# A decoder of two layers on one core: byte codes for four of sixteen heads in a quantised cross-attention, and a later schedule around them

## The chip, the cores and the metric

The kernel runs on one core of a Trainium2 chip. The metric is the device time of the whole program in microseconds, from one launch. Six sublayers are computed in that launch; the change touches mainly the fifth.

## The reference, cut to what matters

`x` is 4 x 256 rows of 256 numbers, so 1,024 queries; `cond` (the context) has as many rows, all of which are keys for every query. There are 16 heads of 16 numbers. What the fifth sublayer computes:

```python
x = x + attn0(ln(x)); x = x + xattn0(ln(x), ctx, ctx); x = x + bitlinear_ffn(ln(x)); x = x + latent_attn(ln(x))
# the fifth: quantised cross-attention
q = (ln(x) @ Wq + bq).reshape(1, B * N, 16, 16) / 4
k, v = split((cond @ Wkv + bkv).reshape(1, -1, 2, 16, 16))
q = fq_sym(q, axis=-1); k = fq_sym(k, axis=-1); v = fq_sym(v, axis=2)   # whole numbers to 127, times a scale
attn = softmax(einsum('bhqd,bhkd->bhqk', q, k))
attn = fq_unsigned(attn, axis=-1)   # round(attn / max * 255), times a scale
x = x + einsum('bhqk,bhkd->bhqd', attn, v).reshape(B, N, C) @ Wp + bp
x = x + moe(ln(x))                  # 32 experts and 32 empty ones, the best 8 of 64 for each token
```

With the row's largest score subtracted and ln 255 added, the exponential rounded to a whole number is the code from 0 to 255 of `fq_unsigned`. The scale drops out with the division by the row's sum.

## The kernel before

Each engine has its own instruction list, written out by hand, with semaphores between them. The fifth sublayer is a loop over units. Unit `n` is one tile of 128 queries (`q = n // 16`, eight tiles) and one head (`h = n % 16`), 128 units in all; 16 units, one tile, are called a round below. In a unit:

- TensorE multiplies the queries with all 1,024 keys: two matmuls of 128x512 (L1204) into one of three pairs of PSUM banks. It waits until the exponential of unit n-3 has been read out of that pair.
- VectorE takes the negated maximum of the 1,024 scores of each row (L1739). The bias of the exponential, that maximum times a scale plus ln 255, is one tiny instruction: VectorE does it for half of the units (L1746), GpSimd (`score_bias`, L619) for the units in `PBIAS`.
- ScalarE takes the exponential and writes the codes as int16 (L876) to one of `YB` buffers `Y5`; it reads out the row sums with it.
- SP issues a DMA transpose of the 128x1024 codes (L453), so that keys lie on partitions, into one of `YB` buffers `PT5`. The codes' bits are then read as float16.
- TensorE multiplies them with the values: eight matmuls with 16 columns (L1214). These are `LAG5` = 6 units behind: TensorE's list has the scores of unit n and then the value products of unit n-6.

In the free places of the loop lies the work on other tiles, hung on `at_unit(n, h)`, which is true h units after a tile's lag (n - LAG5 = 16 q + h). For tile q+2, which is still to come: the output projection of the fourth sublayer (`WO_H` = 4, TensorE L1117), its residual and statistics on VectorE (L1562, L1566, L1568), the norm on GpSimd (`ln_rstd` L589 and L591, `ln_apply` L596), the transpose, the query projection (`Q5_H` = 10), the quantising (`quantise_queries`), a DMA transpose (`query_T`, L440) and the padding of the queries (`pad_queries`, two copies, L627). For tile q-1, which is finished: the division (L1755, L1757), the output projection (`WP_H` = 6, TensorE L1129), the residual, statistics and norm, `store_rows` (L445) and the router's logits. Where a unit has no such work, TensorE multiplies an identity to keep busy (L1262).

Order in the lists matters, since each engine works its own list in order. GpSimd's for a unit n is the bias if n is in `PBIAS`, then, at their units, the norm of the later tile, the padding, the norm of the finished tile, the bias vector of the residual (L601) and the quantising. SP's is the transpose of the codes, then at its unit `store_rows` or `query_T`. VectorE's is the maximum and bias, then the side work. After the last unit come the router (the first six tiles are routed while the last value products run), the lists of tokens for each expert, and the experts.

The third sublayer quantises its hidden tile in five small steps on VectorE (L1479 to L1490) and then tells TensorE with a counter of its own, `qh_ready` (L1492), that it may transpose (L1025).

## Time and profile before

| what | value |
|---|---|
| median of three runs | 571.26 us (570.69 to 577.84) |
| the profiled execution | 572.61 us |
| its span in the trace | 570.9 us |
| busy over the span: PE, DVE, ACT, POOL | 78%, 76%, 57%, 44% |
| the loop of the fifth sublayer, first to last exponential | 237.2 to 434.9 us |
| median time of one DMA transpose of codes, issue to landing | 3.3 us |

The profiled execution is 1.35 us above the median of the runs; its span is 1.7 us shorter than its own time. Busy shares are over all stages. The loop is a third of the span, and the page's 40 slices show DVE at 7 to 9 tenths, ACT at 7 to 9 and DMA at 9 in it.

### The profile page before, as it was taken

What the parts mean: (1) busy time and instruction counts of PE and PEld (TensorE: products, weight loads), DVE (VectorE), ACT (ScalarE), POOL (GpSimd) and SP (SyncE); (2) the same over time, 40 slices, a digit from 0 to 9 for tenths busy, and PEclk for the clock granted to TensorE, in tenths of its full rate; (3) what the DMA queues carried; (4) which work ended last, traced back from release to release, by engine and by line L of the source; (5) the groups of instructions that cost most, each with busy time, mean ns of one, the idle gap of its engine ahead of it and who ended that gap; (6) DMA issues with size and microseconds to landing.
All of it is one profiled execution on the core that took longest, in us unless ns stands there. A gap on an engine that the chain in (4) does not pass through costs nothing.

```text
span 570.9 us, 10775 instructions
## 1 busy us (share of the span) xinstructions
PE 445.7 (78%) x3776; PEld 280.1 (49%) x3776; DVE 431.9 (76%) x892; ACT 322.7 (57%) x607; POOL 250.2 (44%) x367
## 2 busy tenths in 40 slices
PE   2999796677888888578888777787787877877775
PEld 1534562445555566244444444444434436766664
DVE  4697799889689877999999897999798753412246
ACT  1333434545578456488897887889795114434430
POOL 5645210005089466022536263543312148888860
PEclk9996897999899999898999999999799999999999
DMA  8760000000004202299999999999999978995456
GB/s 283 223 242 0 1 2 1 0 1 2 0 1 113 38 1 30 47 181 171 176 191 179 186 180 174 172 181 193 178 185 155 296 229 206 267 229 94 87 84 209
DMA packets 186149, 74.03 MB, mean 130 GB/s; under 512 B 159120, under 2 KB 183632, under 8 KB 186096
## 3 DMA queue, kind: packets, MB, share of 16 engines
q1 hardware_dynamic: 179968, 64.30, 54.2%
q0 software_dynamic: 5040, 8.00, 7.7%
q10 hardware_dynamic: 1088, 1.05, 0.6%
q8 instruction: 30, 0.49, 0.4%
q14 instruction: 23, 0.19, 0.1%
HBM read 27.69 MB, written 7.88 MB: 62 GB/s over the span
## 4 chain that ended last, share of the span: by engine, by line
PE 31%; DVE 23%; issue 16%; POOL 12%; ACT 9%; DMA 7%; SPq 0%; POOLq 0%; DVEq 0%; ACTq 0%
DVE nm L1739 5%; DMA A<-A 5%; DVE AT L1554 5%; ACT A L876 5%; POOL A L675 4%; PE ps L938 3%; POOL sums L685 3%; PE ps L955 3%; PE ps L1129 2%; PE ps L1204 2%; PE ps L1013 2%; PE ps L956 2%; PE ps L1117 2%; PE ps L1031 1%; ACT A L768 1%
## 5 line engine op out<-in xcount | busy, mean ns | idle before, releaser
L876 ACT ACTIVATE A<-ps,b,sq 128x1024 int16<-128x1024 f32 x128 | 153.6, 1205 | 39.2 <-DVE b L1746 24.8
L1739 DVE TENSOR_REDUCE nm<-ps 128x1 f32<-128x1024 f32 x128 | 152.6, 1211 | 6.9 <-PE ps L1204 6.6
L1204 PE MATMUL ps<-big,ctx_sb 128*128 128x512 bf16 x256 | 80.6, 398 | 33.0 <-ACT A L876 30.0
L1214 PEld LDWEIGHTS ps<-VI,A 128*128 128x128 f16 x1024 | 41.5, 97 | 53.6 <-DMA A<-A 34.3
L619 POOL TENSOR_SCALAR b<-nm,sq 128x1 f32<-128x1 f32 x61 | 16.3, 267 | 109.7 <-DVE nm L1739 100.8
L1214 PE MATMUL ps<-VI,A 128*128 128x16 f16 x1024 | 45.2, 170 | 13.7 <-DMA A<-A 13.0
L1811 DVE TENSOR_TENSOR AT<-AT,ps 128x128 f32<-128x128 f32 x32 | 9.2, 288 | 59.0 <-ACT AT L892 48.7
L1204 PEld LDWEIGHTS ps<-big,ctx_sb 128*128 128x128 bf16 x256 | 18.8, 100 | 57.7 <-ACT A L876 44.3
L675 POOL DMA_INDIRECT A<-x_rows,slot_token x32 | 34.9, 1091 | 23.7 <-DVE big L1731 14.2
L685 POOL DMA_INDIRECT sums<-XN,slot_token x24 | 38.7, 1614 | 8.1 <-issue 7.0
L1322 PE MATMUL ps<-A 128*128 128x128 f32 x256 | 34.8, 279 | 3.8 <-issue 1.8
L1262 PE MATMUL ps<-big,identb 128*128 128x256 bf16 x192 | 36.4, 280 | 0.0
L524 POOL TENSOR_SCALAR veps<-mv 128x4 f32<-128x4 f32 x8 | 2.1, 257 | 76.3 <-DVE mv L1360 76.3
L1322 PEld LDWEIGHTS ps<-A 128*128 128x128 f32 x256 | 31.1, 191 | 6.5 <-issue 6.2
L886 ACT ACTIVATE A<-ps 128x256 f32<-128x256 f32 x32 | 12.3, 383 | 38.6 <-PE ps L1312 32.4
L1554 DVE TENSOR_REDUCE AT<-ps 128x4 f32<-128x512 f32 (+1 forms) x32 | 27.8, 950 | 0.4 <-PE ps L1104 0.4
L921 PE MATMUL ps<-identb 128*128 128x512 bf16 x114 | 27.7, 379 | 0.0
L837 ACT ACTIVATE A<-ps 128x768 f32<-128x768 f32 x22 | 16.6, 808 | 15.6 <-PE ps L1143 15.6
L876 ACT ACTIVATION_READ_ACCUMULATOR A<-ps,b,sq 128x1 f32 x128 | 25.3, 198 | 0.0
L1299 PE MATMUL ps<-big 128*128 128x256 bf16 x192 | 23.9, 273 | 0.3 <-DVE big L1805 0.3
L1312 PE MATMUL ps<-identf,A 128*128 128x128 f32 x64 | 13.3, 290 | 13.7 <-DMA A<-x_rows,slot_token 12.8
L606 POOL TENSOR_SCALAR_AFFINE_SELECT A<-A 128x512 f32<-128x512 f32 x22 | 15.5, 708 | 13.9 <-ACT A L837 13.2
(305 smaller groups left out, 1044.9 us busy)
## 6 DMA issues: line engine op xcount, KB each, us to landing
A<-in SPq DMA_DIRECT2D x32, 256.0 KB
A<-in SPq DMA_DIRECT2D x32, 128.0 KB
A<-in SPq DMA_DIRECT2D x2, 1024.0 KB, 14.3
sums<-zeros SPq DMA_DIRECT2D x4, 512.0 KB, 5.0
A<-A SPq DMA_TRANSPOSE x128, 3.3
X<-in SPq DMA_DIRECT2D x1, 1024.0 KB, 6.0
big<-in SPq DMA_DIRECT2D x1, 1024.0 KB, 8.7
ctx_sb<-in SPq DMA_DIRECT2D x1, 1024.0 KB, 13.0
```

Of the source, the lines that this page charges most:

```text
L675: g.indirect_dma_start(out=XE[:, e % 8, :], out_offset=None, in_=x_rows, in_offset=bass.IndirectOffsetOnAxis(ap=slot_token[:, e:e + 1], ax ...
L685: g.indirect_dma_start(out=sums[j % 2], out_offset=bass.IndirectOffsetOnAxis(ap=slot_token[:, e:e + 1], axis=0), in_=YE[:, e % 8, :], in_o ...
L876: a.activation(Y5[:, n % YB, :], ps[:, 2 * ((n + 1) % 3):2 * ((n + 1) % 3) + 2, :], ACT.Exp, scale=sq5[:, q, h:h + 1], bias=b5[:, n % 4:n ...
L921: T.matmul(ps[:, bank, :], identb[:, :], identb[:, :].unsqueeze(1).to_broadcast([P, 4, P]), start=True, stop=True)
L938: last = T.matmul(ps[:, bank, 0:n], XT[:, k, t * P:(t + 1) * P], w[:, k, 0:n], start=(k == 0), stop=(k == KD - 1))
L1204: done = T.matmul(ps[:, 2 * ((n + 1) % 3) + c, :], QT5[:, q % 2, h // 2, h % 2, :], KT5[:, h // 2, c * 512:(c + 1) * 512], start=True, sto ...
L1214: done = T.matmul(ps[:, 6 + q % 2, h * HD:(h + 1) * HD], PT5h[:, m % YB, k, :], VI[:, k, h * HD:(h + 1) * HD], start=(k == 0), stop=(k == 7))
L1262: T.matmul(ps[:, 6 + q % 2, D:2 * D], identb[:, :], KT5[:, 0, 0:D], start=True, stop=True)
L1299: done = T.matmul(ps[:, 4 + c, (t % 2) * D:(t % 2 + 1) * D], HOT[:, i % 2, t * P:(t + 1) * P], YP[:, i % 2, a, :], start=(i == 0 and a == ...
L1322: last = T.matmul(ps[:, 1, f * P:(f + 1) * P], WG[:, e % WS, k, f * P:(f + 1) * P], XET[:, e % 2, k, :], start=(k == 0), stop=(k == KD - 1))
L1554: v.tensor_reduce(MM4[:, 2 * b + t, :].rearrange("p (r c) -> p r c", r=4)[:, :, HD + g], sc[:, :, lo:hi], AX.X, ALU.max, negate=True).then ...
L1739: v.tensor_reduce(nm5[:, n % 4:n % 4 + 1], ps[:, 2 * ((n + 1) % 3):2 * ((n + 1) % 3) + 2, :].rearrange("p a c -> p (a c)"), AX.X, ALU.max, ...
```

## The change

Four heads of each tile, h in `PACK_H` = (2, 4, 6, 13), so 32 of 128 units, write their codes as bytes. The exponential's output is ordered so that a key of one half of a 256-block and its partner 128 further on lie side by side; a pair of bytes is one 2-byte element. The DMA transpose then has 128x512 elements in place of 128x1024 and goes to one of two buffers `PK5`. GpSimd's new `unpack(m)` waits for it and copies the bytes out to the int16 buffer `PT5`, 1,024 elements for each partition, read with a stride of two bytes. It stands in GpSimd's list at n = m + 5, ahead of that unit's bias. TensorE waits for it in place of the DMA.

Further: `YB` and `LAG5` go from 6 to 8, so everything hung on `at_unit` and `PBIAS` moves two units later. VectorE's residuals and GpSimd's norms after the two projections go one unit further (`WO_H + 1`, `WP_H + 1`), while TensorE's projections stay at `WO_H` and `WP_H`. `pad_queries` goes from `WP_H` (6) to 2. In the third sublayer two semaphores are saved by counting on in others, which also removes VectorE's wait and increment of `qh_ready`. The logits' buffer moves in SBUF.

```diff
-YB, LAG5 = 6, 6
+YB, LAG5 = 8, 8
+        Y5b = A[:, 4096:4096 + 512 * YB].bitcast(U8).rearrange("p (b c) -> p b c", b=YB)
+        PK5 = A[:, 13312:13824].bitcast(I16).rearrange("p (s k c) -> p s k c", s=2, k=4)
+        PK5b = A[:, 13312:13824].bitcast(U8).rearrange("p (s k c a) -> p s k c a", s=2, k=4, a=2)
+        PACK_H = (2, 4, 6, 13)
+        PACKED = [n for n in range(U5) if n % H in PACK_H]
 # SP
-                sp.dma_start_transpose(PT5[:, n % YB, :, :], Y5[:, n % YB, :]).then_inc(p5T_loaded[n % YB], 16)
+                if n in PACKED:
+                    j = PACKED.index(n)
+                    if j >= 2:
+                        sp.wait_ge(S["p5U_ready"], j - 1)
+                    sp.dma_start_transpose(PK5[:, j % 2, :, :], Y5[:, n % YB, 0:512]).then_inc(p5T_loaded[n % YB], 16)
+                else:
+                    sp.dma_start_transpose(PT5[:, n % YB, :, :], Y5[:, n % YB, :]).then_inc(p5T_loaded[n % YB], 16)
 # GpSimd
+            def unpack(m):
+
+                j = PACKED.index(m)
+                pool.wait_ge(p5T_loaded[m % YB], 16 * (m // YB + 1))
+                if m >= YB:
+                    pool.wait_ge(S["p5V_done"], m - YB + 1)
+                g.tensor_copy(PT5[:, m % YB, :, :].rearrange("p (k a) c -> p k a c", k=4), PK5b[:, j % 2, :, :, :].rearrange("p k c a -> p k a c")).then_inc(S["p5U_ready"], 1)
-            for n in range(LAG5, U5 + LAG5 + H):
+            for n in range(LAG5 - 1, U5 + LAG5 + H):
+                if n - 5 in PACKED:
+                    unpack(n - 5)
                 if n in PBIAS:
                     score_bias(n)
-                if at == WO_H and ahead:
+                if at == 2 and 1 <= q < NT - 1:
+                    pad_queries(q + 1, n)
+                if at == WO_H + 1 and ahead:
                     ln_rstd("q", q + 2, q + 3)
                     ln_apply("q", q + 2)
-                if at == WP_H:
-                    if 1 <= q < NT - 1:
-                        pad_queries(q + 1, n)
+                if at == WP_H + 1:
 # ScalarE
-                    a.activation(Y5[:, n % YB, :], ps[:, 2 * ((n + 1) % 3):2 * ((n + 1) % 3) + 2, :], ACT.Exp, scale=sq5[:, q, h:h + 1],
+                    codes, scores = Y5[:, n % YB, :], ps[:, 2 * ((n + 1) % 3):2 * ((n + 1) % 3) + 2, :]
+                    if n in PACKED:
+                        codes = Y5b[:, n % YB, 0:1024].rearrange("p (k c a) -> p k a c", k=4, a=2)
+                        scores = scores.rearrange("p x (k a c) -> p (x k) a c", k=2, a=2)
+                    a.activation(codes, scores, ACT.Exp, scale=sq5[:, q, h:h + 1],
 # TensorE
-                    pe.wait_ge(S["qh_ready"], u + 1)
+                    pe.wait_ge(S["qh_step"], 2 * u + 2)
-                    pe.wait_ge(p5T_loaded[m % YB], 16 * (m // YB + 1))
+                    if m in PACKED:
+                        pe.wait_ge(S["p5U_ready"], PACKED.index(m) + 1)
+                    else:
+                        pe.wait_ge(p5T_loaded[m % YB], 16 * (m // YB + 1))
 # VectorE
-                    dve.wait_ge(S["qh_step"], 2 * s + 2)
-                    dve.sem_inc(S["qh_ready"], 1)
-                if at_unit(n, WO_H) is not None and q + 2 < NT:
+                if at_unit(n, WO_H + 1) is not None and q + 2 < NT:
                     side_residual(q + 2, bank, 0, "wo_psum", "xo_ready")
                     side_stats("q", q + 2, "xo_ready", q + 3)
-                if at_unit(n, WP_H) is not None and q >= 1:
+                if at_unit(n, WP_H + 1) is not None and q >= 1:
                     dve.wait_ge(S["xbias_ready"], q)
                     side_residual(q - 1, bank, D, "wp_psum", "xp_ready")
```

## Rows read from the trace of the kernel before

**Rows 1.** Windows, six rounds: us, busy PE, PEld, DVE, ACT, POOL, clock, DMA.

```profile
253.00:404.00 151.00, 118.39 (x1210) 68.38 (x1207) 137.72 (x206) 126.88 (x221) 64.41 (x119) 0.97 1.06 180
```

**Rows 2.** Timeline of SP's queue, 269 to 399 us: start, length, line, operation.

```profile
269.94 1.30 SPq L440 DMA_TRANSPOSE KV<-kpart  x1
...
295.36 1.28 SPq L440 DMA_TRANSPOSE KV<-kpart  x1
...
320.32 1.81 SPq L440 DMA_TRANSPOSE KV<-kpart  x1
322.22 17.43 SPq L453 DMA_TRANSPOSE A<-A  x12
339.70 0.57 SPq L445 DMA_DIRECT2D x_rows<-XN  x1
...
372.78 1.28 SPq L440 DMA_TRANSPOSE KV<-kpart  x1
...
397.44 1.46 SPq L440 DMA_TRANSPOSE KV<-kpart  x1
```

**Rows 3.** One line's instructions, L453: min/median/max ns; then us to landing.

```profile
L453 SPq DMA_TRANSPOSE A<-A x128: 1231/1285/2516, 238.6 to 437.7; - x128
...
DMA to landing us min/median/max: 3.1/3.3/5.9
```

**Rows 4.** Groups by line, 260 to 433 us: busy us, mean ns, idle before.

```profile
L876 ACT ACTIVATE A<-ps,b,sq 128x1024 int16<-128x1024 f32 x110 | 132.0, 1205 | 28.5 <-DVE b L1746 15.2 <-POOL b L619 10.0 <-DMA A<-A 1.9
L1739 DVE TENSOR_REDUCE nm<-ps 128x1 f32<-128x1024 f32 x110 | 131.0, 1211 | 6.7 <-PE ps L1204 6.6
...
L1214 PE MATMUL ps<-VI,A 128*128 128x16 f16 x880 | 38.9, 170 | 11.4 <-DMA A<-A 10.9
...
L619 POOL TENSOR_SCALAR b<-nm,sq 128x1 f32<-128x1 f32 x56 | 15.0, 267 | 89.9 <-DVE nm L1739 81.0 <-ACT A L876 8.9
...
L627 POOL COPY ctx_sb<-KV 64x1024 bf16<-64x1024 bf16 x12 | 12.4, 1036 | 0.7
...
L639 POOL TENSOR_SCALAR kpart<-ktmp 128x256 bf16<-128x256 f32 x6 | 6.6, 1102 | 0.6
...
L1562 DVE TENSOR_TENSOR X<-X,ps 128x256 f32<-128x256 f32 x12 | 5.0, 418 | 5.8 <-PE ps L1117 3.8 <-PE ps L1129 1.9
...
L641 POOL COPY kpart<-kpart 128x512 bf16<-128x512 bf16 x6 | 3.7, 612 | 0.4
```

**Rows 5.** Timeline of DVE around the residual of a later tile.

```profile
298.00 1.22 DVE L1739 TENSOR_REDUCE nm<-ps 128x1 f32<-128x1024 f32 x1
299.97 0.42 DVE L1562 TENSOR_TENSOR X<-X,ps 128x256 f32<-128x256 f32 x1 [0.76 <-PE ps L1117]
...
300.99 1.20 DVE L1739 TENSOR_REDUCE nm<-ps 128x1 f32<-128x1024 f32 x1
```

**Rows 6.** Timeline of PE in the same stretch.

```profile
297.96 1.97 PE L1117 MATMUL ps<-woT,A 128*128 128x256 f32 x8
299.77 0.59 PE L1204 MATMUL ps<-big,ctx_sb 128*128 128x512 bf16 x2
```

**Rows 7.** Timeline of POOL in the same stretch.

```profile
301.16 0.23 POOL L589 TENSOR_SCALAR veps<-mv 128x1 f32<-128x1 f32 x1 [1.59 <-DVE mv L1568]
...
302.15 1.24 POOL L596 TENSOR_SCALAR XN<-X,mv,rstd 128x256 f32<-128x256 f32 x1
...
303.99 2.13 POOL L627 COPY ctx_sb<-KV 64x1024 bf16<-64x1024 bf16 x2
```

**Rows 8.** The page's costliest groups, an exponential that writes four bytes an element.

```profile
L837 ACT ACTIVATE A<-ps 128x768 f32<-128x768 f32 x22 | 16.6, 808 | 15.6 <-PE ps L1143 15.6
```

**Rows 9.** Timeline of DVE after the last unit.

```profile
440.65 0.21 DVE L1666 MATCH_REPLACE8 ctx_sb<-top,ctx_sb 128x64 f32<-128x64 f32 x1
441.37 0.25 DVE L1755 RECIPROCAL r<-sum 128x16 f32<-128x16 f32 x1 [0.51 <-PE ps L1214]
```

**Rows 10.** One line's instructions, L1025: what its engine waited for, us, times.

```profile
  DVEq L1492: 0.9, 1
```

More of the change, by code:

```diff
@@ L7 @@
 I16 = mybir.dt.int16
+U8 = mybir.dt.uint8
 F16 = mybir.dt.float16
@@ L212, in decoder_kernel @@
         r5 = sb("r5", [P, H])
-        LG5 = A[:, 11264:11776].rearrange("p (t e) -> p t e", t=NT)
+        LG5 = A[:, 12288:12800].rearrange("p (t e) -> p t e", t=NT)
         L6, BI6, RP6, MK6 = (ctx_sb[:, 2 * i:2 * i + 2, :].rearrange("p a (t e) -> p (a t) e", e=NROUTE) for i in (3, 0, 1, 2))
@@ L249, in decoder_kernel @@
             s2_psum sm2_step bias2_ready exp2_ready attn2_ready out2_psum
-            q3_step qx_ready qxT_psum qxT_ready h3_psum gelu_ready am3_step qh_step qh_ready qhT_psum qhT_ready out3_psum
+            q3_step qx_ready qxT_psum qxT_ready h3_psum gelu_ready qh_step qhT_psum qhT_ready out3_psum
             low_psum lstats_ready laggr_ready cn_ready cnT_psum cnT_ready upq_psum upk_psum upq_ready upk_ready v4_psum v4_ready
@@ L253, in decoder_kernel @@
             k5T_loaded wo_psum xo_ready xbias_ready x4T_psum x4T_ready q5pad_ready q5_psum uq5_ready q5_step q5i_ready q5T_loaded
-            s5_psum max5_ready bias5_ready pbias5_ready exp5_ready p5V_done r5_ready o5_ready at5T_psum at5T_ready wp_psum xp_ready x5T_psum x5T_ready lg_ready
+            s5_psum max5_ready bias5_ready pbias5_ready exp5_ready p5U_ready p5V_done r5_ready o5_ready at5T_psum at5T_ready wp_psum xp_ready x5T_psum x5T_ready lg_ready
             lg_psum step6 exp6_ready router_ready pos6_psum const6_ready onehot_ready grid_psum diag_ready list_psum list_step list_ready
@@ L1478, in _ @@
                     g3 = G3[:, s % 2, :]
-                    v.tensor_reduce(am3b[:, s:s + 1], g3, AX.X, ALU.max, apply_absolute_value=True).then_inc(S["am3_step"], 1)
-                    dve.wait_ge(S["am3_step"], 4 * s + 1)
-                    v.tensor_scalar(am3b[:, s:s + 1], am3b[:, s:s + 1], EPS, 1.0 / 127, ALU.max, ALU.mult).then_inc(S["am3_step"], 1)
-                    dve.wait_ge(S["am3_step"], 4 * s + 2)
-                    v.reciprocal(qs3b[:, s:s + 1], am3b[:, s:s + 1]).then_inc(S["am3_step"], 1)
-                    v.tensor_scalar(dq3b[:, s:s + 1], am3b[:, s:s + 1], wmean[:, 1:2], None, ALU.mult).then_inc(S["am3_step"], 1)
-                    dve.wait_ge(S["am3_step"], 4 * s + 3)
+                    v.tensor_reduce(am3b[:, s:s + 1], g3, AX.X, ALU.max, apply_absolute_value=True).then_inc(S["q3_step"], 1)
+                    dve.wait_ge(S["q3_step"], 16 + 4 * s + 1)
+                    v.tensor_scalar(am3b[:, s:s + 1], am3b[:, s:s + 1], EPS, 1.0 / 127, ALU.max, ALU.mult).then_inc(S["q3_step"], 1)
+                    dve.wait_ge(S["q3_step"], 16 + 4 * s + 2)
+                    v.reciprocal(qs3b[:, s:s + 1], am3b[:, s:s + 1]).then_inc(S["q3_step"], 1)
+                    v.tensor_scalar(dq3b[:, s:s + 1], am3b[:, s:s + 1], wmean[:, 1:2], None, ALU.mult).then_inc(S["q3_step"], 1)
+                    dve.wait_ge(S["q3_step"], 16 + 4 * s + 3)
                     v.tensor_scalar(g3, g3, qs3b[:, s:s + 1], ROUND, ALU.mult, ALU.add).then_inc(S["qh_step"], 1)
@@ L1767, in _ @@
                     side_stats("r", q - 1, "xp_ready", q)
-                if at_unit(n, WP_H + 1) is not None and q == NT:
+                if at_unit(n, WP_H + 2) is not None and q == NT:
                     route_masked(0, EARLY)
-                if at_unit(n, WP_H + 2) is not None and q == NT:
+                if at_unit(n, WP_H + 3) is not None and q == NT:
                     side_norm("r", q - 1)
```

## The prediction

> **What bounds the kernel now.** The page says that no engine is busy all the time, and its 40 slices say that the fifth sublayer, a third of the span, is the stretch where VectorE, ScalarE and the DMA engines are all near full. Only that loop matters here. I read four views of it.
>
> First the windows [rows 1]: 151.0 us hold 96 units, six rounds, so 25.2 us for a round and 1.58 us for a unit. VectorE is busy 137.7 us of it (91%, 22.95 us for a round), ScalarE 84%, GpSimd 43% (10.7 us for a round). The busiest engine has 2.2 us idle in a round: no cure of a wait can bring more than that.
>
> Second SP's queue [rows 2]. Its rows follow one another nearly without a hole: 12 transposes of codes take 17.43 us, 1.45 us each, though the median row is 1.285 us [rows 3]; the rest is a gap of 0.1 us at each and some of up to 2.5 us. Sixteen make 23.2 us, and with `query_T` (1.3 to 1.8) and `store_rows` (0.57) and their gaps a round of SP's queue takes 25.4 us. From one `query_T` to the sixth, 269.94 to 397.44, five rounds took 127.5 us, 25.5 us each. SP's queue thus sets the average pace; its transposes land 3.3 us after issue [rows 3], so it is the issue that is full, not the latency.
>
> Third, who feels it [rows 4]. The value products on TensorE wait 10.9 us for transposes in 173 us, 1.6 us in a round. VectorE waits 6.6 us for scores and 5.7 us for the two projections. A round in which SP hardly hurt is that from 295.36 to 320.32, 24.96 us, or from 372.78 to 397.44, 24.66 us [rows 2]: about 24.8. So VectorE's own pace lies only 0.7 us below SP's.
>
> Fourth the place where VectorE idles in such a clean round [rows 5, 6]. TensorE does the projection from 297.96 and is free for the next scores only at 299.77. VectorE has ended its maximum at 299.22, waits 0.76 us for the projection, does 1.02 us of residual and statistics and starts the next maximum at 300.99.
>
> **The change part by part**, for one round, then summed over the six rounds that have all of it.
>
> *Half-size transposes, 4 in 16.* The trace has none of 512 columns. Upper end of the saving: half of 1.45 us, 0.72 each; lower end none. I take 0.65, since the row's 1.285 us is far above what the 128 KB `store_rows` takes to issue (0.57, rows 2) and so must grow with the transpose. SP's round falls by 2.6 us to 22.8 us, under VectorE's.
>
> *Lag of 8.* TensorE reaches the value products of n after the scores of n+8, which wait for the exponential of n+5. From the end of exponential n that is 5 x 1.58 = 7.9 us in place of 4.7; less 3.3 for the transpose, SP may be 4.6 us behind instead of 1.4. Together these two take away SP's pace and TensorE's waits: 25.5 to 24.8 us, **minus 0.7 a round, minus 4.4 us** (with a part of the first and last round). Ends: none, and minus 1.6 a round, all of TensorE's waiting.
>
> *Unpacking.* A COPY of 1,024 columns takes 1.036 us and one of 512 takes 0.612 [rows 4], 0.83 ns a column; I take 1.04 us, 1.1 with its gap. Upper end: the two-operation TENSOR_SCALAR at 1.102 us for 256, 4.4 us for 1,024. GpSimd goes from 10.7 to 15.1 us a round, and is no bound. What counts is its order. Unpack(2) stands between the biases of 6 and 7, whose maxima end about 1.2 us apart: bias 7 comes 0.25 us late. Unpack(4) is at n = 9, where the division of the finished tile gives 0.6 us more: not late. Unpack(13) is two units from a bias. Unpack(6) at n = 11 follows the padding.
>
> *Padding at 2 instead of 6.* The copies take 2.13 us [rows 7], at n = 10 behind bias 10; then unpack(6) 1.1; then bias 12. That is 3.6 us where VectorE needs 2.6 for its two maxima and one bias: bias 12 is 1.0 us late. The transpose that it waits for is issued after exponential 6 and needs 0.7 + 1.3 + 3.3 us; maximum 10 ends some 4.5 us after that exponential, so up to 0.8 us more if SP is behind.
>
> *Norm at 5, next bias at 6.* From the statistics to the end of L596 it is 301.16 to 303.39 [rows 7], 2.3 us; before, the next bias came two units later. Now bias 14 waits: 2.4 against 1.2 us, 1.1 us late.
>
> What hides these: bias 12's delay lies under the projection (next item), which holds up the scores of 13 by 1.2 us anyway; bias 14's lies under the 1.02 us of the second residual. With three PSUM pairs an exponential may also be late by about 0.8 us before VectorE starves: the ring of exponential 1.21, scores 0.59, maximum 1.21 and bias 0.27 [rows 4, 6] is 3.3 us, with an estimated 0.4 for the handing over 3.7, against three units of 1.5. I take 0.1 a round, plus 0.7 us. Ends: nothing; all in full, 0.25 + 1.0 + 1.1 = 2.4 a round, plus 14 us.
>
> *Residual a unit later.* The projection still blocks TensorE, so the next scores end at 300.36 [rows 6]. VectorE would then start its maximum at 300.4, 0.6 us sooner than now, having idled 1.2 us instead of 0.76, and pay the 1.02 us of side work a unit later, when it is full. Net plus 0.43 a round, for six rounds **plus 2.6 us**. Ends: plus 4; and minus 4.6, if it only removes the 0.76. The second residual waits for nothing in a clean round and costs nothing moved.
>
> *Byte output of the exponential.* An exponential writing 4 bytes takes 808 ns for 768 [rows 8], 1.05 ns an element, against 1.18 with 2 bytes [rows 4]: size of output shows no price. I take none. Cover: ScalarE's 16% idle, 4 us a round. Upper end, doubled: 4.8 a round.
>
> *After the last unit.* VectorE routes six tiles until 440.86 and then waits 0.51 us for the last value product [rows 9]; only this can be won, and TensorE's fillers grow by two units. Zero, ends ±0.5. *Third sublayer.* TensorE's transposes waited for that counter once, 0.9 us [rows 10], else the fillers covered it: minus 0.2, ends 0 and minus 0.9.
>
> Sum: -4.4 + 0.7 + 2.6 - 0.2 = -1.3 us. The profiled execution took 572.61 us, so 571.3; the median of the runs is 1.35 lower: **570.0 us**.
>
> **The skill against the rows.** A COPY shows 0.83 ns a column [rows 4]. The Trainium skill, GPSIMD Engine Reference, section 3.1, speaks against the change: it counts about 2.6 cycles an element on GpSimd beside 1 on VectorE, though 1.03 for bodies of at most two operands. By the 2.6 an unpack would be an estimated 2.2 us; by the sum's own steps biases 7 and 12 then come 1.1 us later still, some +8 us. The rows of COPY bear out the 1.03. A unit moves 262 KB in 1.45 us of SP's time, 181 GB/s [rows 2]. The same skill, Advanced Engine Details and Errata, X-Bar Transpose, says that such transposes are as fast as other DMAs, at 350 to 400 GB/s; by that the queue would have had no pace to lose and the sum would be +3.1 without the -4.4. The rows contradict it.
>
> **The rivals.**
> - *VectorE gets all of it.* The waits for scores go and the residual's wait too: 0.7 x 6.3 + 4.6 = 9 us, 562 us. For: VectorE has 2.2 us idle a round. Against: the projection keeps TensorE for 1.8 us wherever the residual is put [rows 6].
> - *GpSimd's queue takes SP's place* (slower). Unpacking, padding and norm stand ahead of biases 7, 12 and 14, and each delay goes on to ScalarE, the scores and VectorE: +14 with -4.4 and +2.6, 583 us. It passes 2% at 1.9 us lost a round, net; an unpack of 1.04 us needs all its delays in full for that, one of over 2.2 us would do it with half. For: GpSimd waits for VectorE before nearly every bias [rows 4], so a bias is always urgent. Against: the slack above.
> - *Half as many elements, as long to issue.* SP stays at 25.4 us a round and binds; the lag only gives tolerance, and the residual's cost hides under SP: 571 us. For: no row shows a smaller transpose.
>
> **How the numbers follow.** My forecast 0.50 (566 to 576); VectorE gets all 0.22; GpSimd's queue 0.17; same issue time 0.11. The range is 562 to 583: below it lies the tail of the first rival, above it the worse half of the second. Two per cent, about what a measurement of this kernel tells from no change, is 11.4 us. Faster by more needs 1.9 us a round, nearly all of VectorE's idle: 0.03. Slower by more: 0.10. Within: 0.87.
>
> **What would show it.** Rows of half-size transposes near 0.65 us and holes in SP's queue; value products that never wait for a DMA; a COPY of 1.04 us; VectorE's maximum after the projection starting 1.2 us after the one before ended, with the residual behind it; biases 7, 12 and 14 late but the round at 25.3 us. Wrong if the unpack is far above 1.04 us, if ScalarE's byte exponentials are longer than 1.2 us, or if a round is under 24.5 us.

## The result, and the profile after

The changed kernel took 587.17 us, the median of four runs (582.75 to 589.71), against 573.0 for the kernel before on the same chip (the three runs above and a fourth of 574.74); the ratio is 1.0238 with the 95% interval [1.0187, 1.029]. The forecast was 570.0 us in a range of 562 to 583, so it was wrong in sign and the time lies above the range. The profiled execution is the fastest of the four, 582.75 us with a span of 581.0; it shows 10.1 us of the loss. From first to last exponential the loop took 208.3 us, 234.6 to 442.9, against 197.6: 10.7 us more. It began 2.6 us earlier, and after it came 138.1 us instead of 136.0.

Counted from exponential 15 to 111 in steps of sixteen, the six full rounds took 27.7, 27.7, 27.9, 25.4, 27.4 and 26.4 us; before they took 25.4, 24.7, 25.5, 27.4, 24.7 and 26.2. The window that answers to [rows 1] shows all three busy engines less busy, and the granted clock lower (columns as there):

```profile
253.00:404.00 151.00, 118.30 (x1100) 72.44 (x1120) 127.12 (x195) 115.01 (x201) 83.53 (x135) 0.89 0.86 149
```

TensorE does 1,100 matmuls in place of 1,210 in the same busy time, at a mean clock of 0.89 in place of 0.97. The DMA share fell from 1.06 to 0.86. VectorE is idle for 23.9 us instead of 13.3.

SP's queue, answering to [rows 2] (timeline of SP; L464 is the half-size transpose, L466 the full one), and the instructions of its two lines, answering to [rows 3]:

```profile
301.33 1.26 SPq L447 DMA_TRANSPOSE KV<-kpart  x1
302.68 8.22 SPq L466 DMA_TRANSPOSE A<-A  x6
311.00 1.97 SPq L464 DMA_TRANSPOSE A<-A  x1
313.67 5.37 SPq L466 DMA_TRANSPOSE A<-A  x4
...
329.93 1.26 SPq L447 DMA_TRANSPOSE KV<-kpart  x1
```

```profile
L464 SPq DMA_TRANSPOSE A<-A x32: 1188/1210/2442, 238.7 to 444.3; - x32
...
DMA to landing us min/median/max: 2.4/2.5/4.2
```

```profile
L466 SPq DMA_TRANSPOSE A<-A x96: 1231/1280/2297, 235.9 to 446.9; - x96
```

Half as many elements take 1.21 us to issue, not 0.65; only the landing is earlier, 2.5 us for 3.3. There are holes in the queue now, but they are a follower's: SP waits for exponentials that come late.

The groups by line, 260 to 433 us, answering to [rows 4]:

```profile
L1767 DVE TENSOR_REDUCE nm<-ps 128x1 f32<-128x1024 f32 x104 | 123.5, 1212 | 23.3 <-PE ps L1231 23.0
L903 ACT ACTIVATE A<-ps,b,sq 128x1024 int16<-128x1024 f32 x77 | 92.3, 1204 | 26.6 <-POOL b L632 24.5 <-DVE b L1774 1.0
...
L1244 PE MATMUL ps<-VI,A 128*128 128x16 f16 x827 | 36.9, 171 | 1.5 <-POOL A L662 1.5
...
L903 ACT ACTIVATE A<-ps,b,sq 128x1024 uint8<-128x1024 f32 x27 | 32.5, 1204 | 2.3 <-DVE b L1774 1.6 <-POOL b L632 0.2
L662 POOL CAST A<-A 128x1024 int16<-128x1024 uint8 x25 | 25.9, 1036 | 1.2
...
L1156 PE MATMUL ps<-wp,A 128*128 128x256 f32 x24 | 6.8, 404 | 3.9 <-DVE X L1590 3.9
...
L1149 PE MATMUL ps<-identf,XN 128*128 128x128 f32 x22 | 5.2, 322 | 4.2 <-DVE X L1590 4.2
...
L1590 DVE TENSOR_TENSOR X<-X,ps 128x256 f32<-128x256 f32 x11 | 4.5, 411 | 0.0
...
L884 ACT ACTIVATE AT<-ps 128x256 f32<-128x256 f32 x6 | 2.3, 383 | 8.7 <-PE ps L1156 8.7
```

Read against [rows 4]: the value products no longer wait for a DMA (1.5 us, for an unpack, where it was 10.9), and the residual no longer waits at all (5.8 before). But VectorE's maxima wait 23.0 us for scores instead of 6.6, ScalarE waits 24.5 us for GpSimd's biases instead of 10.0 (for VectorE's it waits less, so that its waits for all biases are 27.3 us against 25.2 and hardly grew), and there are three waits that the trace of before did not have: TensorE waits 3.9 us ahead of `wp` and 4.2 us ahead of the transposes of the later tile, both times for **VectorE's residual** (L1590), and ScalarE waits 8.7 us for the query projection.

One round shows where they stand. TensorE's timeline, answering to [rows 6] (the projection `woT` at 304.73 is the one of 297.96 there):

```profile
304.73 1.97 PE L1144 MATMUL ps<-woT,A 128*128 128x256 f32 x8
...
309.02 1.13 PE L1156 MATMUL ps<-wp,A 128*128 128x256 f32 x4 [0.86 <-DVE X L1590]
...
312.53 0.44 PE L1149 MATMUL ps<-identf,XN 128*128 128x128 f32 x2 [0.91 <-DVE X L1590]
313.92 0.63 PE L1231 MATMUL ps<-big,ctx_sb 128*128 128x512 bf16 x1 [0.95 <-ACT A L903]
...
316.18 1.22 PE L1154 MATMUL ps<-bqr,onesf 1*128 1x256 f32 x2
317.33 2.08 PE L1156 MATMUL ps<-wq,A 128*128 128x256 f32 x4
319.20 1.06 PE L1231 MATMUL ps<-big,ctx_sb 128*128 128x512 bf16 x2
```

VectorE's in the same stretch, answering to [rows 5], and then GpSimd's, answering to [rows 7]:

```profile
307.17 1.23 DVE L1767 TENSOR_REDUCE nm<-ps 128x1 f32<-128x1024 f32 x1 [1.19 <-PE ps L1231]
...
308.56 0.41 DVE L1590 TENSOR_TENSOR X<-X,ps 128x256 f32<-128x256 f32 x1
...
320.30 1.23 DVE L1767 TENSOR_REDUCE nm<-ps 128x1 f32<-128x1024 f32 x1 [2.73 <-PE ps L1231]
```

```profile
304.19 2.12 POOL L640 COPY ctx_sb<-KV 64x1024 bf16<-64x1024 bf16 x2 [0.36 <-POOL b L632]
306.38 1.04 POOL L662 CAST A<-A 128x1024 int16<-128x1024 uint8 x1
307.51 0.27 POOL L632 TENSOR_SCALAR b<-nm,sq 128x1 f32<-128x1 f32 x1
...
312.05 0.26 POOL L632 TENSOR_SCALAR b<-nm,sq 128x1 f32<-128x1 f32 x1
```

TensorE is at `wp` at 308.16 and stands until VectorE has read the bank of `woT`, 0.86 us; two units later the same again, 0.91 us for the residual of `wp`; then 0.95 us for an exponential. ScalarE began that exponential at 312.35, after waiting 2.06 us for GpSimd's bias of 312.05, and this bias stood behind a norm that had waited 1.97 us for VectorE's late statistics. So the third wait too can come from the later residual, by way of GpSimd. Then every TensorE instruction is nearly twice as long: the matmuls of `wq` 2.08 us where the four of before took 1.13 in each of the six rounds, the scores 1.06 for 0.59. The windows of this round (columns as in [rows 1]; the clock is the third from the end) say why:

```profile
303.00:313.60 10.60, 7.81 (x79) 5.32 (x78) 9.17 (x16) 7.41 (x14) 6.20 (x11) 1.00 1.06 170
313.90:320.70 6.80, 6.78 (x40) 3.88 (x40) 3.87 (x7) 4.83 (x9) 3.13 (x4) 0.50 0.81 154
320.70:330.70 10.00, 7.20 (x86) 4.31 (x87) 9.82 (x15) 8.47 (x17) 5.95 (x11) 1.00 0.67 107
```

For 6.8 us the granted clock is 0.50, the 1.2 GHz level; TensorE is busy 6.78 us of them and VectorE only 3.87. Five of the six rounds have `wq` at 2.08 us, a mean of 27.4 us; the other, the fourth in order, has it at 1.13 and took 25.4. The waits ahead of it are not alike in all six. Four of the five slow ones have the two waits for residuals at 0.81 to 0.91 us. The first has no finished tile yet and so no `wp`; there TensorE waits 1.24 us for the later tile's norm. In the fourth the two waits are shorter (TensorE's timeline):

```profile
256.64 0.41 PE L1149 MATMUL ps<-identf,XN 128*128 128x128 f32 x2 [1.24 <-POOL XN L609]
...
336.88 1.13 PE L1156 MATMUL ps<-wp,A 128*128 128x256 f32 x4 [0.47 <-DVE X L1590]
...
340.39 0.44 PE L1149 MATMUL ps<-identf,XN 128*128 128x128 f32 x2 [0.60 <-DVE X L1590]
```

In all, the loop has 37.5 us at half clock in six stretches; before it had 17.1 in four, none of them over a query projection.

The three small ones. The exponential that writes four bytes is as [rows 8] had it, 808 ns each; the last division, which answers to [rows 9], waits for nothing now, but comes later, since routing ends at 450.46; and TensorE's wait in the third sublayer, answering to [rows 10], is 0.8 us for 0.9:

```profile
450.25 0.21 DVE L1694 MATCH_REPLACE8 ctx_sb<-top,ctx_sb 128x64 f32<-128x64 f32 x1
450.56 0.25 DVE L1783 RECIPROCAL r<-sum 128x16 f32<-128x16 f32 x1
```

```profile
  DVE A L1520: 0.8, 1
```

### The profile page after: what moved, and what is told of

Its sections match the earlier page's. It is cut to its first block, busy times and chain, and to the rows that moved or that the text cites. A ratio compares the mean times of both kernels' runs of the same rounds, so it can differ in the third digit from the quotient of the medians.

```text
span 581.0 us, 10818 instructions
## 1 busy us (share of the span) xinstructions
PE 448.6 (77%) x3760; PEld 288.8 (50%) x3792; DVE 431.8 (74%) x892; ACT 322.6 (56%) x607; POOL 283.1 (49%) x399
## 4 chain that ended last, share of the span: by engine, by line
PE 35%; DVE 21%; issue 15%; POOL 13%; ACT 7%; DMA 6%; SPq 1%; POOLq 0%; DVEq 0%; ACTq 0%
DVE AT L1582 5%; DVE nm L1767 4%; PE ps L965 3%; PE ps L1231 3%; PE ps L982 3%; PE ps L1156 3%; ACT A L903 3%; POOL A L662 2%; PE ps L1144 2%; DMA A<-x_rows,slot_token 2%; PE ps L948 2%; POOL sums L708 2%; DMA sums<-XN,slot_token 2%; PE ps L1352 2%; PE ps L1040 2%
## 5 line engine op out<-in xcount | busy, mean ns | idle before, releaser
L903 ACT ACTIVATE A<-ps,b,sq 128x1024 int16<-128x1024 f32 (+1 forms) x128 | 153.5, 1204 | 41.6 <-POOL b L632 27.7
L1767 DVE TENSOR_REDUCE nm<-ps 128x1 f32<-128x1024 f32 x128 | 152.2, 1213 | 25.1 <-PE ps L1231 24.6
L1231 PE MATMUL ps<-big,ctx_sb 128*128 128x512 bf16 x227 | 77.1, 413 | 41.4 <-ACT A L903 37.0
L1244 PEld LDWEIGHTS ps<-VI,A 128*128 128x128 f16 x1024 | 45.4, 98 | 36.9 <-issue 7.5
L662 POOL CAST A<-A 128x1024 int16<-128x1024 uint8 x32 | 33.2, 1037 | 16.1 <-DMA A<-A 14.7
L1292 PE MATMUL ps<-big,identb 128*128 128x256 bf16 x208 | 39.0, 282 | 0.0
L913 ACT ACTIVATE A<-ps 128x256 f32<-128x256 f32 x32 | 12.2, 382 | 40.1 <-PE ps L1342 40.0
L948 PE MATMUL ps<-identb 128*128 128x512 bf16 x114 | 29.4, 397 | 0.0
L1342 PE MATMUL ps<-identf,A 128*128 128x128 f32 x64 | 13.4, 292 | 16.1 <-DMA A<-x_rows,slot_token 15.5
L903 ACT ACTIVATION_READ_ACCUMULATOR A<-ps,b,sq 128x1 f32 x128 | 25.4, 198 | 0.0
L1329 PE MATMUL ps<-big 128*128 128x256 bf16 x192 | 23.9, 273 | 0.1
## 6 DMA issues: line engine op xcount, KB each, us to landing
ctx_sb<-in SPq DMA_DIRECT2D x1, 1024.0 KB, 13.4
```

The lines of the kernel that those rows point to most:

```text
L662: g.tensor_copy(PT5[:, m % YB, :, :].rearrange("p (k a) c -> p k a c", k=4), PK5b[:, j % 2, :, :, :].rearrange("p k c a -> p k a c")).then ...
L903: a.activation(codes, scores, ACT.Exp, scale=sq5[:, q, h:h + 1], bias=b5[:, n % 4:n % 4 + 1], accum_out=sum5[:, n:n + 1]).then_inc(S["exp5 ...
L948: T.matmul(ps[:, bank, :], identb[:, :], identb[:, :].unsqueeze(1).to_broadcast([P, 4, P]), start=True, stop=True)
L1231: done = T.matmul(ps[:, 2 * ((n + 1) % 3) + c, :], QT5[:, q % 2, h // 2, h % 2, :], KT5[:, h // 2, c * 512:(c + 1) * 512], start=True, sto ...
L1244: done = T.matmul(ps[:, 6 + q % 2, h * HD:(h + 1) * HD], PT5h[:, m % YB, k, :], VI[:, k, h * HD:(h + 1) * HD], start=(k == 0), stop=(k == 7))
L1292: T.matmul(ps[:, 6 + q % 2, D:2 * D], identb[:, :], KT5[:, 0, 0:D], start=True, stop=True)
```

## The experiments

The theories, with the letters that the expectations use. **A**, GpSimd's list: unpack, padding and norm ahead of biases make the loss. **B**, the residual a unit later: TensorE waits for it, its clock drops, the rest follows. **C**, SP's issue was the pace before, and a half-size transpose saves only 0.07 us of it. The kernels are the changed one with the edit shown, unless it says otherwise; `...` in an edit stands for lines left out. "Ratio" is the kernel's time over that of the kernel before on the same chip, whose median was 572.9 to 574.9 us, with its 95% interval; "loop" is the time from first to last exponential in the profiled execution; `wq` is the query projection, 1.13 us at full clock and 2.08 at half. A clean round is one of the shortest that come back in a loop, near 24.6 us.

Wherever VectorE's residuals go back to their old units, the first routing steps after the loop (`route_masked` and the two behind it) go back by one unit of VectorE's list too.

### Everything but the lag taken back

```diff
-        PACK_H = (2, 4, 6, 13)
+        PACK_H = ()
-                if at == 2 and 1 <= q < NT - 1:
-                    pad_queries(q + 1, n)
-                if at == WO_H + 1 and ahead:
+                if at == WO_H and ahead:
-                if at == WP_H + 1:
+                if at == WP_H:
+                    if 1 <= q < NT - 1:
+                        pad_queries(q + 1, n)
-                if at_unit(n, WO_H + 1) is not None and q + 2 < NT:
+                if at_unit(n, WO_H) is not None and q + 2 < NT:
-                if at_unit(n, WP_H + 1) is not None and q >= 1:
+                if at_unit(n, WP_H) is not None and q >= 1:
...
```

> The changed kernel without packing (all 128 units in int16, no unpack) and with residuals, norms and padding at their old units (4, 6 and 6 after the lag); what stays of the change is the lag of 8 with 8 buffers and the third sublayer's semaphores. Theory A (the loss is made in GpSimd's list by unpack, padding and norm ahead of biases 12 and 14): no loss, 568 to 573 us, since GpSimd's list is the old one. Theory B (the loss is made by the residual a unit later, for which TensorE's next side work waits, with the clock falling after it): the same, 568 to 573. Theory C (SP's issue was the pace before and a half-size transpose saves only 0.07 us of it): the round stays at 25.3 to 25.5 us, so 571 to 573. If it is slower than 576, the lag itself costs something that none of them has.

Ratio 1.0143 [1.0044, 1.0241], loop 202.2 us. A wait of its own stands in the waits of 260 to 433 us (engine and line, what it waited for: us, times, longest):

```profile
PE ps L1231 <- POOL ctx_sb L640: 16.8, 6, 3.0
```

The scores wait for the padded queries. With a lag of 8, unit 6 after the lag is only two units ahead of the next tile's first scores; with 6 it was four. So the padding at 2 is not a free move: the lag needs it. The clock drops here as well, with the residuals in their place: 23.9 us of the loop are at half clock and two of six `wq` at 2.08. None of the expected times (568 to 573 us) came; the median was 581.23.

### Only the packing taken out

```diff
-        PACK_H = (2, 4, 6, 13)
+        PACK_H = ()
```

> The changed kernel without packing alone: all units int16, no unpack; lag 8, residuals and norms a unit later and padding at 2 as changed. Theory A with unpack as the cause: bias 12 then stands behind the padding only and is on time, bias 14 stays late behind the norm; some 3 to 6 us of the 14 come back, 579 to 583 us. Theory B: nothing comes back, 585 to 588, since TensorE's waits at the two projections have nothing to do with packing. Theory C: SP gets no slower by more than 4 x 0.07 us a round, so it does not bind at 27 us a round.

Ratio 1.0161 [1.0063, 1.026], loop 205.6 us, four of six `wq` at 2.08. Most of the loss stays without any packing, so the unpack of theory A is not what makes it. Whether a few us of it are the packing's can't be told: the interval reaches over 1.0238. Two neighbouring rounds of its TensorE timeline:

```profile
312.68 1.13 PE L1156 MATMUL ps<-wp,A 128*128 128x256 f32 x4 [0.86 <-DVE X L1590]
...
316.19 0.44 PE L1149 MATMUL ps<-identf,XN 128*128 128x128 f32 x2 [0.91 <-DVE X L1590]
...
319.89 1.13 PE L1156 MATMUL ps<-wq,A 128*128 128x256 f32 x4
...
338.36 1.13 PE L1156 MATMUL ps<-wp,A 128*128 128x256 f32 x4 [0.85 <-DVE X L1590]
...
341.87 0.44 PE L1149 MATMUL ps<-identf,XN 128*128 128x128 f32 x2 [0.91 <-DVE X L1590]
...
346.54 2.08 PE L1156 MATMUL ps<-wq,A 128*128 128x256 f32 x4
```

The same two waits stand ahead of a `wq` at full and of one at half clock. They make the drop likely, not certain; why this round escapes stays open. The other round that escapes here, the one before it, had the second wait at 0.45 us.

### The packing, with side work and padding at the old units

```diff
-                if at == 2 and 1 <= q < NT - 1:
-                    pad_queries(q + 1, n)
...
+                    if 1 <= q < NT - 1:
+                        pad_queries(q + 1, n)
-                if at_unit(n, WO_H + 1) is not None and q + 2 < NT:
+                if at_unit(n, WO_H) is not None and q + 2 < NT:
...
```

> The changed kernel with packing and unpack as they are, but residuals, norms and padding at their old units. Theory A with unpack as the cause: the unpacks of 2 and 6 still stand ahead of biases, the norm and padding no longer do: 574 to 578 us. Theory B: the whole loss is gone, 570 to 573 us. If the round falls under 24.8 us and the time under 568, packing was worth something and only the rest spoiled it.

Ratio 1.0117 [1.0027, 1.0207], loop 203.9 us, and again 16.9 us of scores waiting for the padding in six times. Theory B expected the whole loss gone, 570 to 573 us, and the median was 582.67. As with the lag alone, the late padding spoils the reading; the next two have it at 2.

### Residuals and norms at their old units, padding at 2

```diff
-                if at == WO_H + 1 and ahead:
+                if at == WO_H and ahead:
-                if at == WP_H + 1:
+                if at == WP_H:
-                if at_unit(n, WO_H + 1) is not None and q + 2 < NT:
+                if at_unit(n, WO_H) is not None and q + 2 < NT:
-                if at_unit(n, WP_H + 1) is not None and q >= 1:
+                if at_unit(n, WP_H) is not None and q >= 1:
...
```

> The changed kernel with residuals on VectorE and norms on GpSimd back at 4 and 6; packing, lag 8 and the padding at 2 (followed by the unpack of unit 6, then bias 12, then the norm of the later tile) as changed. Theory B: the loss is gone, 570 to 573 us. Theory A: bias 14 is no longer behind the norm by much, but bias 12 is still 1.1 us late behind padding and unpack: 577 to 581 us. Against e3 the difference is the padding's place alone.

Ratio 0.9976 [0.9935, 1.0017], loop 195.9 us, every `wq` at 1.13, 13.7 us at half clock. The whole loss is gone with residuals and norms back. The waits, as above:

```profile
ACT A L903 <- POOL b L632: 21.4, 27, 3.5
...
DVE nm L1767 <- PE ps L1231: 2.6, 10, 0.5
```

ScalarE still waits 21.4 us for GpSimd's biases, nearly as in the changed kernel, yet VectorE waits only 2.6 us for scores and the clean rounds take 24.6 us. A falls: the late biases are there and are hidden. Theory B's 570 to 573 us is met.

### The same without packing

```diff
-        PACK_H = (2, 4, 6, 13)
+        PACK_H = ()
```

> No packing and no unpack; lag 8, residuals and norms at 4 and 6, padding at 2. Against e4 (572.8 us, ratio to before 0.998) the difference is the packing alone. Theory A (unpack in GpSimd's list costs): up to 1 us a round better than e4, 567 to 570 us. Theory C (SP's issue is the pace again once the other losses are gone, and packing relieves it only by 0.07 us for each transpose but takes the wait for a free DMA engine away): the round is 25.3 us again, 572 to 575 us. Against e1 (581 us) it measures the padding at 6 behind a lag of 8: 8 to 10 us.

(The edit is to the kernel just above.) Ratio 0.9985 [0.9938, 1.0031], loop 195.2 us. With packing it was 0.9976: the packing is worth nothing that can be measured. SP's queue is full again, and the two rounds from 283.2 to 332.7 us still take 24.9 and 24.6 (timeline of SP):

```profile
298.90 17.25 SPq L466 DMA_TRANSPOSE A<-A  x12
```

So a queue with sixteen full-size transposes a round keeps up with 24.6 us; it does not by itself hold a round at 25.4 or 25.5. Theory C's time came (573.06 in 572 to 575 us) and so, as a mean, did its round (25.2 us for 25.3), but with packing the mean is 25.3 too, so SP's issue is not what makes it.

### TensorE kept busy in its waits

```diff
+                    for c in range(4 if n < U5 else 0):
+                        T.matmul(ps[:, 6 + q % 2, D:2 * D], identb[:, :], KT5[:, 0, 0:D], start=True, stop=True)
                     wait_side_read(pe, side - 1)
...
```

Four identity matmuls of 256 columns ahead of the wait for `wp`, four ahead of that for the transposes of the later tile and four behind these.

> The changed kernel entire, with four filler matmuls of 256 columns on TensorE ahead of each of its two waits for a residual's read (before the second projection and before the transposes of the later tile) and four behind those transposes. Theory B2 (the residual a unit later costs mainly because these waits are followed by TensorE's clock at half): the query projection is again 1.1 us and not 2.1, the rounds of 27.6 us become 25.4 to 25.8, and the time 576 to 580 us. Theory B1 (the waits themselves and the late bias are the cost, and the clock follows from them without effect): 584 to 590 us, since the fillers only add work.

Ratio 1.0117 [1.0033, 1.02], loop 197.6 us, every `wq` at 1.13, rounds of 25.4 five times and then 23.6. The residual is still late, but the clock holds (window, columns as in [rows 1]; then VectorE's idle time in one round):

```profile
303.00:330.00 27.00, 22.46 (x232) 13.68 (x233) 24.72 (x37) 22.64 (x42) 16.58 (x27) 1.00 0.93 158
```

```profile
308.80 1.23 DVE L1773 TENSOR_REDUCE nm<-ps 128x1 f32<-128x1024 f32 x1 [1.19 <-PE ps L1231]
...
319.47 1.23 DVE L1773 TENSOR_REDUCE nm<-ps 128x1 f32<-128x1024 f32 x1 [0.56 <-PE ps L1231]
```

In the loop 3.4 us are at half clock, against 37.5, and the loop is 10.7 us shorter than in the changed kernel: the clock was the larger part of the loss. The fillers also lie in the waits and shorten what is left of them, to 0.36 to 0.46 us. A smaller part is left with the clock at full: VectorE waits 12.2 us for scores in 260 to 433 us, and the rounds take 25.4 us where clean ones with the residual in place take 24.6. What it costs the whole program is less sure. The loop is as long as that of the kernel before, and of the 5.6 us by which this span (576.5) exceeds that one (570.9), 3.7 us lie ahead of the loop, where the fillers and the later residual do nothing.

### VectorE's residuals back, GpSimd's norms still late

```diff
-                if at_unit(n, WO_H + 1) is not None and q + 2 < NT:
+                if at_unit(n, WO_H) is not None and q + 2 < NT:
-                if at_unit(n, WP_H + 1) is not None and q >= 1:
+                if at_unit(n, WP_H) is not None and q >= 1:
...
```

> The changed kernel with only VectorE's two residuals back at the units of their projections; GpSimd's norms stay a unit later. Theory B (TensorE waits for the residual's read, clock after it): the loss is gone, 570 to 575 us. Theory A (norm ahead of bias 14 is what costs): bias 14 is ready only after the norm at n = 13, which now can start a unit earlier, right behind bias 12, so it is late by at most a few tenths: also most of it back, but the transposes of the later tile may wait: 573 to 578 us.

Ratio 0.9974 [0.9927, 1.0021], loop 194.9 us. Of the two engines whose side work moved, it is VectorE's that costs; GpSimd's late norms cost nothing by themselves. This is the best kernel of the study, and its interval still holds 1.

### The late bias given to VectorE

```diff
-        PBIAS_AT = (0, 1, 2, 4, 6, 11, 14, 15)
+        PBIAS_AT = (0, 1, 2, 6, 9, 11, 14, 15)
```

Added to the kernel with residuals and norms at their old units: the bias that comes behind padding and unpack is VectorE's.

> e4 (packing, lag 8, padding at 2, residuals and norms at their old units) with the bias of unit 12, which GpSimd reaches 2 to 3 us late behind padding and unpack, done by VectorE, and that of unit 17 by GpSimd instead. Theory A: the gap of 3.9 us before exponential 12 falls to some 2.7 and a round from 25.1 to 24.2 us: 565 to 569 us. If VectorE is the bound and hides the delay, the same as e4, 571 to 574 us.

Ratio 1.0003 [0.996, 1.0046]. Its profiled execution took 579.69 us, above its own median of 573.27, so only the order of its waits is read. ScalarE waits for GpSimd 9.4 us instead of 21.4, but 15.6 for VectorE:

```profile
ACT A L903 <- DVE b L1774: 15.6, 16, 2.8
ACT A L903 <- POOL b L632: 9.4, 22, 1.5
```

The gap goes from unit 12 to unit 13, and the clean rounds stay at 24.6 us. One of its six `wq`, at 391.85, takes 2.07 us: a drop over the query projection can also come with the residual in its place.

### The kernel before with late residuals and norms

```diff
-                if at_unit(n, WO_H) is not None and q + 2 < NT:
+                if at_unit(n, WO_H + 1) is not None and q + 2 < NT:
-                if at_unit(n, WP_H) is not None and q >= 1:
+                if at_unit(n, WP_H + 1) is not None and q >= 1:
-                if at == WO_H and ahead:
+                if at == WO_H + 1 and ahead:
...
```

Lag 6, no packing, padding at `WP_H`; norms and residuals a unit later (and the third sublayer's counters as changed).

> The kernel before in all but one thing: lag 6 and 6 buffers, no packing, padding at 6, but VectorE's residuals and GpSimd's norms a unit after their projections (and the third sublayer's semaphores of the change). Theory B (the residual a unit later is the cause by itself): TensorE waits 0.8 to 0.9 us at the second projection and at the transposes in each round, its clock falls after it in most rounds, 580 to 587 us. If it needs the lag of 8 or the packing beside it, 571 to 575 us.

Ratio 1.0198 [1.0125, 1.0271], loop 210.7 us, five of six `wq` at 2.08, 41.0 us at half clock. The move whose return undoes the loss is also enough to make it. No run moves the residuals without the norms. The waits of 260 to 433 us:

```profile
DVE nm L1767 <- PE ps L1231: 23.8, 16, 2.7
...
PE ps L1149 <- DVE X L1590: 4.3, 5, 0.9
```

They are close to those of the changed kernel, 23.0 and 4.2; the wait ahead of `wp` is 2.1 us in all instead of 3.9, and the clock drops all the same.

### The kernel before with the packing alone

```diff
-YB, LAG5 = 8, 8
+YB, LAG5 = 6, 6
...
```

This with residuals, norms and padding at their old units, so lag 6 with packing and unpack.

> The kernel before with packing and unpack alone: lag 6, residuals, norms and padding as before. Theory C (a half-size transpose still takes 1.21 us of SP's queue, and the unpack of 1.04 us lies between its landing and the value products): SP saves 0.3 us a round, the packed units' values come 2.5 + up to 1.1 us and GpSimd's place in line after issue, so TensorE waits for unpack where it waited for the transpose: 572 to 578 us. The rule of the prediction (0.65 us saved each) would give 566 to 569.

Ratio 1.0651 [1.0597, 1.0706], loop 233.7 us, the worst of all, far above the 572 to 578 us expected. One wait stands out, and 58.8 us of the loop are at half clock:

```profile
PE ps L1244 <- POOL A L662: 44.8, 21, 4.1
```

GpSimd's unpack of m stands at m + 5, behind the norm and the padding, and TensorE wants it at m + 6. The lag of 8 is what makes the packing bearable; it bought nothing else that the runs can tell.

### The best of both

```diff
+                    for c in range(4 if n < U5 else 0):
+                        T.matmul(ps[:, 6 + q % 2, D:2 * D], identb[:, :], KT5[:, 0, 0:D], start=True, stop=True)
...
-                if at_unit(n, WO_H + 1) is not None and q + 2 < NT:
+                if at_unit(n, WO_H) is not None and q + 2 < NT:
...
```

> e7 (VectorE's residuals back, the rest of the change kept) with the fillers of e6 ahead of the second projection and around the later tile's transposes. If rounds longer than 24.6 us in e7 come from the clock, all are 24.6 to 24.8 us and the time is 566 to 569 us, 3 to 4 below e7's typical run; if they come from transposes that SP issues slowly, no change: 569 to 573.

(The fillers and the edit of VectorE's residuals, both to the changed kernel.) Ratio 1.0007 [0.9977, 1.0036], loop 199.1 us, every `wq` at 1.13. No gain over 0.9974: with the residual in its place there was no drop over the query projection to prevent. Neither expectation came. The rounds are not all 24.6 to 24.8 us but 23.6 to 28.2, and 13.7 us of the loop are still at half clock, so what makes the rounds longer than 24.6 stays open.

### And ten biases on GpSimd

```diff
-        PBIAS_AT = (0, 1, 2, 4, 6, 11, 14, 15)
+        PBIAS_AT = (0, 1, 2, 6, 9, 10, 11, 13, 14, 15)
```

> e11 with ten biases of a round on GpSimd in place of eight, and none of them right behind the padding. If VectorE's list is the floor of a round once the waits are gone, 0.44 us less of it each round: 24.2 us, 2 to 3 us below e11. If the floor is the ring through exponential, scores and maximum, no change from e11, or worse by late biases.

(Added to the kernel just above.) Ratio 1.0009 [0.9971, 1.0046]. Two more biases off VectorE make 0.4 us a round (two of 0.21), and nothing of it is seen: the rounds are 24.0 us and longer, four of the six from 24.9 to 25.8. VectorE's list thus does not by itself set the pace of a round; which engine or ring does is not shown.

### The four corners

The residual's place and the filling of TensorE's waits together, as ratios to the kernel before:

| | waits not filled | waits filled |
|---|---|---|
| VectorE's residual a unit later | 1.0238 [1.0187, 1.029] | 1.0117 [1.0033, 1.02] |
| VectorE's residual in place | 0.9974 [0.9927, 1.0021] | 1.0007 [0.9977, 1.0036] |

Late costs 0.0264 without fillers, 15 us, and 0.0110 with them, 6 us. The difference of some 9 us is what the fillers take back, and with them the half clock goes (37.5 to 3.4 us). By the intervals the 15 and the 6 are each uncertain by 4 to 5 us and their difference by some 6; the clock's records and the length of `wq` do not depend on them.

The loops of the four profiled executions are 208.3 and 197.6 us in the upper row, 194.9 and 199.1 in the lower. They agree with the 15 and the 9 (13.4 and 10.7 us) and not with the 6: with fillers the loop with the late residual is the shorter one. What is seen of the later order itself is the clean round, 25.4 instead of 24.6 us; a loss of 6 us by it is not shown.

## Why the prediction was wrong, step by step

- **The step that failed: "The second residual waits for nothing in a clean round and costs nothing moved", and with it "plus 2.6 us" for the residual a unit later.** It counted VectorE's side only. Who waits for the residual was in the code: TensorE reuses the side banks and calls `wait_side_read` ahead of `wp` and of the next transposes. A unit later, the residual ends behind TensorE's arrival, and each move costs TensorE 0.86 and 0.91 us. The upper end of plus 4 knew only VectorE's 1.02 us; the runs show 15 us by the four corners, 10.7 of them given back in the loop when fillers keep the clock up.
- *The first residual.* Its own part of the step was right in form: VectorE waited 1.19 us for scores after the projection (1.2 said) instead of 0.76, and paid the side work later. The price on TensorE, 0.86 us ahead of `wp`, was missed here too.
- *The clock* was in no step. The trace of before showed it at 0.97 in the loop and dips of 17.1 us. Shown: the fillers, which change nothing in what waits for what, take `wq` from 2.08 to 1.13 us. That the waits alone decide when the clock drops is not shown: with the packing out, one round kept the full clock behind the same 0.86 and 0.91 us. The Trainium skill, TensorE: Matmul & The Clock Gate, in the section HAM oscillation, tells of a matmul loop in which TensorE waits for a DMA in each pass and starts each next pass throttled. Here the waits are for other engines and under 1.3 us each; the drop comes back in five rounds of six, not in all.
- *Half-size transposes*, 0.65 us each saved: 0.07 (1.210 for 1.280). The lower end, none, was right. `store_rows` was no yardstick: it is another kind of DMA.
- *SP's pace and the lag*, minus 4.4: the waits of the value products did go, 10.9 to 1.5 us, by the lag and not by the packing. The lag with padding at 2 alone gives 0.9985, minus 0.9 us with an interval from minus 3.6 to plus 1.8; its loop is 2.4 us shorter in the profiled execution. So mis-sized, and perhaps nothing. The premise that SP's queue sets the pace at 25.4 to 25.5 us failed as well: with the packing out, rounds of 24.9 and 24.6 us have all sixteen full-size transposes.
- *Unpack*, 1.04 us: 1.036, right. The Trainium skill, GPSIMD Engine Reference, section 3.1, has 2.6 and 1.03 cycles an element, and 1.2 GHz; for 1,024 elements that is an estimated 2.2 or 0.88 us, and the measured cast lies near the second. The section gives the 2.6 to a `tensor_tensor` with two inputs and the 1.03 to "k ≤ 2" without saying what k counts, so the prediction's "at most two operands" is not what it says.
- *Padding at 2* was costed as a lateness of bias 12. That was so and hidden (with residuals in place ScalarE waits 2.17 us for bias 12 in a round of 24.6). What it prevents, 8 to 9 us with a lag of 8 (1.0143 against 0.9985, 1.0117 against 0.9976), was not seen.
- *Norm at 5*, bias 14 late by 1.1: the bias at 312.05 came 1.3 us after its maximum ended (the first of the two from 309.56, in VectorE's timeline), and ScalarE waited 2.06 us for it. Hidden too: with the norms late and only VectorE's residuals back the ratio is 0.9974. The estimate of plus 0.7 for all that GpSimd delays is not contradicted, and is too small to be measured here. With the residual late, though, this late bias stands ahead of TensorE's third wait of 0.95 us, which no step had.
- *Byte exponentials*, none: 1,204 ns with one byte and with two. Right.
- *After the last unit*, zero and ends of 0.5: 2.1 us longer, 138.1 for 136.0. Routing begins three units of the list later (lag and `WP_H + 2`) and ends 7.6 us after the last exponential instead of 6.0.
- *Third sublayer*, minus 0.2: the wait is 0.8 us for 0.9. The loop begins at 234.6 to 241.0 us in changed kernels that are alike up to there, so no such price can be read.
- *The rivals.* VectorE gets all: its waits grew. GpSimd's queue takes SP's place: nearest in time, 583, and wrong in its mechanism as far as it stands alone, for the late biases are still there when the loss is gone. Same issue time for half the elements: its premise is what the rows show, but the residual's price did not hide under SP.

## What to carry to other kernels

Before an engine's read of a shared bank is moved later, look for who overwrites that bank next, and price the wait there, not on the engine that moves. A few waits of under 1 us on TensorE can be followed by a stretch at half clock that costs more than the waits; look for it in the trace wherever the loop repeats them. Parts that go together should be priced together: here padding at 2 and a lag of 8 are one move, and packing without that lag loses 6.5%.

## What the runs showed of the hardware

- The issue of a DMA transpose hardly differs between the two sizes here: 1.21 us for 128x512 two-byte elements, 1.28 for 128x1024; the landing took 2.5 and 3.3 us.
- Three TensorE waits of 0.81 to 0.86, 0.91 and 0.95 to 0.97 us within 6 us were followed by 6.8 us at a granted clock of 0.50 in all four rounds of the changed kernel that have them; a round with 0.47, 0.60 and 0.95 kept the full clock. In the kernel without packing, a round with 0.86, 0.91 and 0.73 kept it and the next, with 0.85, 0.91 and 0.73, did not. With twelve identity matmuls of 256 columns a round around these waits the loop had 3.4 us at half clock in all instead of 37.5.
- ScalarE's exponential takes 1,204 ns for 1,024 elements a partition whether it writes two bytes in order or one byte in interleaved order.
